# A triangular recurrence on VectorE and TensorE: the columns of two neighbouring steps added on VectorE before TensorE subtracts them

## The reference, cut to what matters

```python
def step(Sst, inp):
    qt, kt, vt, bt, gt = inp
    Sd = gt[..., None, None] * Sst
    kS = jnp.einsum('bhk,bhkv->bhv', kt, Sd)
    Snew = Sd + jnp.einsum('bhk,bhv->bhkv', kt, bt[..., None] * (vt - kS))
    ot = jnp.einsum('bhk,bhkv->bhv', qt, Snew)
    return (Snew, ot)
```

## Time and profile before

| what | value |
|---|---|
| median of three runs | 885.64 us |
| the profiled execution, its own time | 881.1 us |
| its span, first to last instruction | 879.4 us |
| mean granted TensorE clock | 0.977 |
| busy: TensorE, VectorE, ScalarE, GpSimd | 793.7, 614.7, 391.3, 183.5 us |
| the recurrence: first row copied to last product of TensorE | 185.15 to 307.7 us |

### The profile page before, as it was taken

The page is one execution under the profiler, slowest core; times in us unless marked ns, Lnnn a source line. Parts: engine busy times, 40 slices in busy tenths (PEclk is TensorE's granted clock), DMA queues, the critical chain, the costliest instruction groups (busy, mean ns, idle before and its releaser), DMA issues.

```text
span 879.4 us, 19821 instructions
## 1 busy us (share of the span) xinstructions
PE 793.7 (90%) x7700; PEld 586.2 (67%) x7700; DVE 614.7 (70%) x976; ACT 391.3 (45%) x561; POOL 183.5 (21%) x197
## 2 busy tenths in 40 slices
PE   4998978989986988977798998799999999999997
PEld 3665757944543666755487885477777777777775
DVE  5796697678787386898767977767777655545544
ACT  5344764610224143666457965334444432323332
POOL 7000790006999801000402420000000000000000
PEclk9999979999999999999999999799999999999999
DMA  8000000020000000010130001144444322222221
GB/s 310 1 2 1 3 1 3 3 96 1 0 0 1 0 2 1 1 39 1 37 78 14 22 21 38 57 127 158 154 150 154 109 68 57 70 69 69 68 61 51
DMA packets 24073, 46.07 MB, mean 52 GB/s; under 512 B 2605, under 2 KB 10541, under 8 KB 23629
## 3 DMA queue, kind: packets, MB, share of 16 engines
q1 hardware_dynamic: 24013, 45.21, 16.8%
HBM read 41.91 MB, written 1.36 MB: 49 GB/s over the span
## 4 chain that ended last, share of the span: by engine, by line
PE 70%; DVE 21%; ACT 4%; issue 3%; POOL 1%; DMA 1%; SPq 0%; DVEq 0%; ACTq 0%; POOLq 0%
PE psum L1790 11%; PE psum L1791 11%; PE psum L1792 11%; PE psum L1982 6%; PE psum L1992 4%; PE psum L828 4%; PE psum L829 4%; PE psum L830 4%; PE psum L2124 1%; DVE arena L1460 1%; PE psum L2170 1%; DVE arena L1658 1%; PE psum L1963 1%; PE psum L2187 1%; PE psum L2156 1%
## 5 line engine op out<-in xcount | busy, mean ns | idle before, releaser
L1790 PE MATMUL psum<-xh,arena 128*128 128x296 f16 (+1 forms) x664 | 193.3, 291 | 8.3 <-DVE xl L1333 5.0
L1791 PE MATMUL psum<-xl,arena 128*128 128x296 f16 (+1 forms) x664 | 193.2, 291 | 0.0
L1792 PE MATMUL psum<-xh,arena 128*128 128x296 f16 (+1 forms) x664 | 193.2, 291 | 0.0
L697 DVE TENSOR_TENSOR arena<-arena 128x592 f16<-128x592 f32 x68 | 52.7, 775 | 61.1 <-ACT arena L608 60.8
L603 ACT ACTIVATE arena<-psum 128x592 f32<-128x592 f32 x66 | 43.8, 664 | 115.7 <-PE psum L1792 115.7
L1790 PEld LDWEIGHTS psum<-xh,arena 128*128 (+2 forms) x664 | 65.3, 98 | 30.8 <-DVE xl L1333 4.5
L752 DVE TENSOR_TENSOR arena<-psum,arena 128x592 f32<-128x592 f32 x64 | 49.6, 775 | 50.8 <-PE psum L1792 50.6
L828 PE MATMUL psum<-arena 128*128 128x296 f16 x272 | 79.9, 294 | 4.6 <-DVE arena L697 3.8
L608 ACT ACTIVATE arena<-arena 128x592 f16<-128x592 f32 x66 | 46.0, 696 | 77.6 <-DVE arena L691 74.8
L829 PE MATMUL psum<-arena 128*128 128x296 f16 x272 | 79.9, 294 | 0.0
L830 PE MATMUL psum<-arena 128*128 128x296 f16 x272 | 79.8, 293 | 0.0
(11 more groups left out here) (321 smaller groups left out, 1675.3 us busy)
## 6 DMA issues: line engine op xcount, KB each, us to landing
arena<-comb SPq DMA_DIRECT2D x62, 296.0 KB, 3.3
arena<-in_wmoe SPq DMA_DIRECT2D x34, 384.0 KB, 3.0
arena<-in_xt SPq DMA_DIRECT2D x4, 864.0 KB, 9.6
arena<-in_w SPq DMA_DIRECT2D x2, 1024.0 KB, 6.6
arena<-arena SPq DMA_DIRECT2D x6, 187.0 KB
arena<-in_ctrl SPq DMA_DIRECT2D x1, 1056.0 KB, 9.1
out<-arena SPq DMA_DIRECT2D x2, 512.0 KB, 3.1
arena<-in_wlin SPq DMA_DIRECT2D x1, 768.0 KB, 4.4
```

Of the source, the lines that this page charges most:

```text
L697: dve.tensor_tensor(al[:, s_], t1, ah[:, s_], ALU.subtract).then_inc(ev["al"], 1)
L1790: pe.matmul(dst, wh, mh, start=start, stop=False)
L1791: pe.matmul(dst, wh, ml, start=False, stop=False)
L1792: return pe.matmul(dst, wl, mh, start=False, stop=stop)
```

## The change

In groups 0 and 1 the steps 0 to 5 and 8 to 13 are taken in pairs (0 and 1, 2 and 3, 4 and 5, and likewise in group 1). The first step of a pair writes its column for the later groups into a ring slot and tells nobody. The second writes its column into a scratch slot, waits for it, adds it to the first with a `tensor_tensor` between two tiles of SBUF, and then signals TensorE, which makes one set of subtractions for both. Steps 6, 7, 14 and 15 and everything from step 16 on are as before. The ring has two slots, and the third one's memory is the scratch slot. The counts of semaphores follow. ScalarE, GpSimd and the DMAs are not touched.

```diff
-RING, QRING = 3, 3
+RING, QRING = 2, 3
+def in_pair(s_):
+    return s_ < 16 and s_ % 8 < 6
+
+def first_of_pair(s_):
+    return in_pair(s_) and s_ % 2 == 0
...
-        ring = carve(0, RING, 64 * (S - 8))
+        ring = carve(0, RING + 1, 64 * (S - 8))
...
-            return sum(len(GROUPS) - 1 - x // 8 for x in range(s_)) + g - s_ // 8
+            return sum(len(GROUPS) - 1 - x // 8 for x in range(s_) if not first_of_pair(x)) + g - s_ // 8
...
-            added_after = [added_by(s_, hi - 1) for s_ in range(S) for _, hi in later_ops(s_)]
+            added_after = [added_by(s_, hi - 1) for s_ in range(S) if not first_of_pair(s_) for _, hi in later_ops(s_)]
...
                 for lo, hi in later_ops(s_):
-                    if n_ >= RING:
+                    slot, t0, t1 = ring[:, n_ % RING], GROUPS[lo][0], GROUPS[hi - 1][1]
+                    if n_ >= RING and (first_of_pair(s_) or not in_pair(s_)):
                         dve.wait_ge(ev["added"], added_after[n_ - RING])
-                    column(dve, ring[:, n_ % RING], 0, s_, GROUPS[lo][0], GROUPS[hi - 1][1], u).then_inc(ev["later"], 1)
+                    if first_of_pair(s_):
+                        link(column(dve, slot, 0, s_, t0, t1, u), hold=False)
+                        continue
+                    if in_pair(s_):
+                        link(column(dve, ring[:, RING], 0, s_, t0, t1, u))
+                        both = slot[:, 0:64 * (t1 - t0)]
+                        dve.tensor_tensor(both, both, ring[:, RING, 0:64 * (t1 - t0)], ALU.add).then_inc(ev["later"], 1)
+                    else:
+                        column(dve, slot, 0, s_, t0, t1, u).then_inc(ev["later"], 1)
                     n_ += 1
...
-                for lo, hi in later_ops(s_) if s_ < S else []:
+                for lo, hi in later_ops(s_) if s_ < S and not first_of_pair(s_) else []:
                     pe.wait_ge(ev["later"], n_ + 1)
```

## The result

The changed kernel takes 899.16 us (four runs, 896.49 to 900.85) against 885.34 for the kernel before in the same comparison: a ratio of 1.0154 with a 95% interval of 1.0127 to 1.0180, or 13.8 us more. 896.2 was forecast, with 889.5 to 902.5 for 8 cases in 10. The profiled execution took 900.85 us, the highest of its four runs, for a span of 899.1; that of before took 881.1, under all its timed runs. So the two traces lie 19.7 us apart where the medians lie 13.8 apart, and each stretch has to be looked at by itself.

A forecast was written before the change was run, and what follows sets the result against it. TensorE was taken to bound groups 0 and 1, VectorE close behind. Group 0 4.8, group 1 0.2, port 3.9 and clock 1.7 made +10.6 us, 896.2 us on the median of 885.64; range 889.5 to 902.5 for 8 in 10.

The forecast's parts named there:

- The adds' price: Six VectorE adds at 1.044 ns a column: 2.09 us each in group 0, 1.56 us each in group 1.
- Group 0, +4.8 us: Row 8 comes 4.8 us later: 6.4 us of adds get back 1.6 us of what TensorE was behind.
- Group 1, +0.2 us: Rows 8 to 16 take 30.3 us against 30.07; the adds get back TensorE's 4.6 us.
- The port, +3.9 us: Adds with two SBUF operands wait for GpSimd: 1.2 us each in group 1, 0.3 for group 0's third.
- The clock, +1.7 us: Gaps on TensorE halve its clock in group 0, 1.7 us (0 to 3.1); nothing taken in group 1.
- The sum: 4.8 + 0.2 + 3.9 + 1.7 = +10.6 us at row 16.
- So the end moves by as much: Behind row 16 the work is the same, so the kernel's end moves by row 16's +10.6 us.
- 64 us from row 16 to TensorE's last product: Sign in the profile after: the stretch behind row 16 stays at 64 us as before.
- A: Rival: the adds alone, port costs nothing and clock holds; +5.0 us, 890.6; chance 0.22 with its neighbours.
- B: Rival: TensorE at 1.2 GHz through both groups, each add waits a full product; +18.2, 903.8; chance 0.14.
- C: Rival: no change, VectorE's 10.6 us idle takes in the 11.2 us of adds; 885 to 887; chance 0.04.
- D: Rival: faster, the adds run at a higher rate than the rows give; 885.0 at twice the rate; chance 0.03.

The follow-up runs named there:

- Filling the gaps: The changed kernel with small bf16 matmuls in TensorE's gaps of groups 0 and 1: 896.11 us, ratio 1.0174 to the kernel before.
- without the port: The changed kernel with the second operand of each add taken from PSUM, not SBUF: 895.88 us, ratio 1.0158 to the kernel before.
- the kernel with both cures: The changed kernel with one add operand in PSUM and small matmuls in TensorE's gaps: 890.03 us, ratio 1.0087 to the kernel before.
- one pair: The kernel before with a single pair, steps 12 and 13, and three ring slots: 882.57 us, ratio 1.0013 to the kernel before.

## Why the prediction was right, point by point

**The bound.** Right: both groups had TensorE last, and VectorE close behind with room only at the ends of the groups. With 16 us less on TensorE and no adds the kernel gains 0.2%, and the interval takes in no gain.

**The adds' price.** Right: 2.09 and 1.56 us where GpSimd is out of the way, as worked out from L1597.

**Group 0, +4.8 us.** Right, at +5.1: 33.28 us with port and clock taken out, 33.0 to 33.5 expected. The wait for the slot of step 6 (2.42 us) is there, and a second one that had not been named, 2.25 us for the slot of the third pair, since that pair was subtracted at half rate. The wait for the slot of step 6 is the ring's: row 8 was ready by 221.05 us, when TensorE's subtractions begun at 212.00 had ended, and was copied at 222.17. One thing was not seen: the 28.18 us of before hold 1.7 us of half rate themselves, as the 26.49 us of other kernels without pairs there show. Against a start at full clock the pairs of group 0 cost that much more.

**Group 1, +0.2 us.** Mis-sized: +1.4 us (31.46 against 30.07). The step "TensorE has three things ahead of row 16" took it to be up to date when step 14's column comes. It has a pair and a Q column of 3.7 us to do in the 2.8 us until then.

**The port, +3.9 us.** The mechanism was right. On VectorE it cost 2.1 us (0.42 + 1.04 + 0 + 0.65). One of the three adds in group 1 met GpSimd idle, waiting 3.44 us for a slot of `qring`, which had not been reckoned with. GpSimd itself lost 3.6 us (3.00, 2.59 and 2.98 against 1.67); up to row 16 that held nothing up.

**The clock, +1.7 us.** Filling the gaps gave 3.1 us in the profile. The 1.7 us of group 0 are as forecast. In group 1 I took nothing, on the ground that 5.4 of 8 us busy had kept the clock; there the gaps ahead of the first and the last pair are 4.1 and 2.8 us long, and both started at 0.50.

**Port and clock together.** How the two divide depends on the order in which they are taken out. Up to row 16 the changed kernel takes 70.18 us, without the port 66.43, with the gaps filled 67.06, with both 64.74. Clock first, it is 3.1 and then 2.3 us of port; port first, it is 3.75 and then 1.7 us of clock, which are the forecast's 3.9 and 1.7. So only their sum, 5.4 us against a forecast of 5.6, is a test, and it holds.

**The sum.** 6.5 us of adds (5.0 forecast) and 5.4 of port and clock (5.6) make the 11.9 us to row 16, where 10.6 were forecast. The median says 13.8.

**Behind row 16: the step that failed.** "So the end moves by as much" put at nothing, without a reason, what the change does behind row 16. The work there is the same, but its start is not: with two slots the second part of column 15 and the reduction behind it come late, GpSimd's product follows 1.8 us later after row 16, and rows 19 to 22 take 11.73 us for 9.95. With it the profiles give 13.7 us, by the median of 13.8. The prediction's own sign for this step, 64 us from row 16 to TensorE's last product, failed too: it took 66.4 us, and 64.3 before. The forecast held because 3.2 us too little lay inside a range that reached from 6.7 us below it to 6.3 above; 899.16 stands 0.3 us under the upper end of the likeliest's own range.

**The rivals.** A (the adds alone) is what the kernel with both cures shows, 7.7 us and not 5.0: 6.5 us up to row 16, and the ring's 1.8 behind it. B (half rate all through) did not come: the clock was at 0.85 and 0.86. C is out by the slot waits that stayed at the groups' ends (2.42 and 2.96 us) and by the ratio; D by the adds' length in the profile.

## What to carry to other kernels

An engine that is busy all through a stretch is not a bound worth unloading by itself: ask how much idle time the engine that takes the work has, and where. Here VectorE's 10.6 us lay at two ends of groups, and 11.2 us of adds within the steps got back only 4.7 us of it (6.5 us were left). Before moving work to VectorE, look at what GpSimd does at that time and whether the new instruction has both operands in SBUF. And count what the unloaded engine loses: TensorE got gaps, and with them half its clock just where the next row waited for it. Count too what the memory was for: the third ring slot, given up for the scratch column, was what let VectorE and then GpSimd run ahead at the ends of the groups. By the profiles that is about 3 of the 13.8 us, an estimate from the 1.1 us between row 8 being ready and being copied and the 1.8 us between rows 19 and 22; no run took it out.

## What the runs showed that I had not expected

The start of the recurrence varies by itself. In kernels with three slots and no pairs in group 0, row 0 to row 8 took 26.49 to 28.18 us, by how long TensorE stays near 1.2 GHz behind a gap of 3.65 us. In the two with two slots it took 29.25 and 30.14, with the ring's 0.8 us in it.

The turns at the port are one-sided here: GpSimd's products, which had begun ahead of the add, kept their length (1.52 us for the one begun at 228.24), the add waited, and the Q column behind them paid for the whole rest of the add (3.00 us for 1.67).

A gain of 3 us in one profile (one pair: 115.25 us from row 0 to row 36 against 118.21) can be half luck: 1.7 of it was the clock between rows 28 and 32, which falls or holds in kernels that are alike there. And the part behind row 36, the same program, took 575.9 to 582.0 us over fourteen profiled executions. A stretch that recurs to 0.05 us, such as rows 19 to 22, is worth more than either.
